# One scan call for both states of a step in every half, the norms' epsilon on GpSimd, half 0's softplus by blocks, and new places in a hand-written order

## The reference, cut to what matters

```python
dt = jax.nn.softplus(einsum('btk,kd->btd', dt, dt_proj_w) + dt_proj_b)
A_bar = exp(dt[..., None] * A)                 # 512 channels x 16 states
Bx = dt[..., None] * B_t * x_branch[..., None]
h = a * h + bx;  y = einsum('bds,bs->bd', h, c)   # for each of 1024 times
...
def _layernorm(x): return (x - mean) / sqrt(var + eps)
```

## Time and profile before

| | |
|---|---|
| three runs | 1342.04, 1348.8 (median), 1353.73 us |
| profiled execution | 1350.41 us, span 1349.1 us |
| mean granted TensorE clock | 0.959 |
| busy: PE, DVE, ACT, POOL | 1162.8, 1219.4, 818.3, 979.5 us |
| first scan | 117.3 us after the span's start |
| the eight halves, from first scan to first scan | 155.2, 149.0, 146.4, 149.0, 149.8, 149.0, 142.3 us, then 191.2 us to the end |

### The profile page before, as it was taken

The page is one execution under the profiler, slowest core; times in us unless marked ns, Lnnn a source line. Parts: engine busy times, 40 slices in busy tenths (PEclk is TensorE's granted clock), DMA queues, the critical chain, the costliest instruction groups (busy, mean ns, idle before and its releaser), DMA issues.

```text
span 1349.1 us, 12381 instructions
## 1 busy us (share of the span) xinstructions
PE 1162.8 (86%) x3574; PEld 639.5 (47%) x3574; DVE 1219.4 (90%) x1338; ACT 818.3 (61%) x1476; POOL 979.5 (73%) x528
## 2 busy tenths in 40 slices
PE   7666967998999899998899898999899899769884
PEld 5423523473446543663357443654357344423453
DVE  4656899999999999899999998899999999989976
ACT  3236645865677666955686675865686577545422
POOL 3203894799769887889679978899589978856742
PEclk9777988899999999999999999999999999989998
DMA  7305557776777669766877668776877677787811
GB/s 257 118 5 206 219 202 242 273 246 213 253 248 242 242 226 307 263 251 209 274 240 272 219 244 266 270 244 202 276 244 253 225 260 252 271 332 271 330 63 78
DMA packets 92020, 313.87 MB, mean 233 GB/s; under 512 B 10400, under 2 KB 15648, under 8 KB 91696
## 3 DMA queue, kind: packets, MB, share of 16 engines
q1 hardware_dynamic: 88928, 303.77, 64.8%
q10 hardware_dynamic: 3024, 9.31, 1.8%
HBM read 301.73 MB, written 11.31 MB: 232 GB/s over the span
## 4 chain that ended last, share of the span: by engine, by line
DVE 39%; PE 22%; issue 13%; ACT 9%; DMA 8%; POOL 8%; SPq 1%; DVEq 0%; POOLq 0%; ACTq 0%
DVE ps L1637 10%; DVE ps L1629 9%; DMA arena<-bc_scratch 7%; DVE arena L1642 6%; PE ps L844 6%; POOL arena L1851 5%; PE ps L550 4%; DVE ps L1345 4%; ACT ps L1203 3%; DVE stats_before L1238 2%; PE ps L590 1%; ACT arena L859 1%; PE ps L596 1%; PE ps L685 1%; DMA arena<-in_x 1%
## 5 line engine op out<-in xcount | busy, mean ns | idle before, releaser
L1851 POOL TENSOR_TENSOR arena<-arena 128x1024 f32<-128x1024 f32 x255 | 597.1, 2360 | 182.2 <-PE ps L844 142.6
L844 PE MATMUL ps<-arena,identF 128*128 128x512 f32 x1024 | 489.2, 610 | 50.1 <-DVE arena L1642 26.9
L1203 ACT ACTIVATE ps<-arena,negA 128x512 f32<-128x512 f32 x512 | 332.6, 683 | 102.6 <-DVE arena L1642 97.5
L1637 DVE TENSOR_TENSOR_SCAN ps<-ps,arena 128x512 f32<-128x512 f32 x258 | 316.9, 1273 | 12.1 <-ACT ps L1203 8.7
L844 PEld LDWEIGHTS ps<-arena,identF 128*128 128x128 f32 x1024 | 190.8, 194 | 283.8 <-issue 218.3
L1642 DVE TENSOR_TENSOR arena<-ps,arena 128x1024 f32<-128x1024 f32 x256 | 312.2, 1219 | 12.6 <-DMA arena<-bc_scratch 6.9
L1629 DVE TENSOR_TENSOR_SCAN ps<-ps,arena 128x1024 f32<-128x1024 f32 x127 | 290.6, 2288 | 19.6 <-ACT ps L1203 17.8
L1655 POOL TENSOR_TENSOR rnln<-vnln,consts 128x4 f32<-128x4 f32 x32 | 33.4, 1044 | 85.5 <-DVE vnln L1254 85.5
L859 ACT ACTIVATE arena<-arena,rnln 128x256 f32<-128x256 f32 x128 | 66.3, 588 | 40.1 <-POOL rnln L1657 40.0
L596 PE MATMUL ps<-arena,inw 128*128 128x512 f32 x128 | 63.9, 647 | 21.3 <-DVE arena L1351 12.1
L439 PE MATMUL ps<-identF,arena 128*128 128x128 f32 x248 | 38.6, 300 | 50.6 <-ACT arena L859 24.8
...
## 6 DMA issues: line engine op xcount, KB each, us to landing
arena<-bc_scratch SPq DMA_DIRECT2D x512, 512.0 KB, 5.0
...
```

The costliest lines, as they stand in the source:

```text
L844: x = pe.matmul(ps[:, Y, :], identF[:], inp[:, m % 4, q, :], start=False, stop=(i == BLOCK_STEPS - 1 and q == 1), skip_group_check=True)
L1203: x = act.activation(ps[:, 2 * (m % 2) + q, :], dt[:, kd, :], ACT.Exp, scale=negA[:, kd, 2 * i + q:2 * i + q + 1])
L1637: x = dve.tensor_tensor_scan(states, states, inp[:, m % 4, q, :], first, ALU.mult, ALU.add)
L1851: pool.tensor_tensor(inp[:, m % 4, :, :], u[:, kd:kd + 1, :].broadcast_to([P, 2, TH]), b_at[:, m % 3, :, :], ALU.mult).then_inc(S.inp, 1)
```

## The change

1. **Scans.** `together(m)` is gone. Every step but step 0 makes one scan of 1024 with initial value 0; step 0 makes two of 512. dt of time 0 is set to LONG in every half. The state carried into an odd half is instead multiplied by the decay of time 0 and added to time 0 of `inp`: ACT makes exp(A * dt[0]) for a pair of blocks (`act_first_decay`, two calls of 128x16, twice per odd half), POOL multiplies `carried` by it (128x32, twice per odd half), and after each `inp` of an odd half POOL adds two columns (128x2), after waiting for its own multiplication. `S.inp` is counted after that add. In all halves ACT's decay of blocks 0 and 2 waits for `S.dt_cut`, so for `u`, in odd halves for the product with `carried` too.
2. **Epsilon.** `dve_veps` is gone; `pool_rstd` makes the two small instructions itself, ahead of the power.
3. **Half 0.** x_proj comes ahead of the dt product on PE for each block. ACT makes |x|, exp and ln for blocks 0 and 1 alone, ln in two calls; DVE adds, multiplies `u` and `inp` for block 0 alone; the row loads of step 0 are split in two. Block 1's add, `u` and cut, and blocks 2 and 3's |x| (now on DVE) and relu, follow at step 1, ACT's exp at step 1 and ln at step 4, POOL's add at step 6 (before: step 4).
4. **Output loads.** Half 0 set: due at 4, 6, 8, ... 14 (before 4.25, 5.25, ... 9.25); half 1 set at 17, 19, ... 27 (before 19.25, ... 24.25); gate loads a quarter step apart.
5. **Places.** Nearly every entry of `TIMES` moves by 0.25 to 3 steps.

```diff
-    "sp_before": {"x_in": -5.75, "bc_out": 29.25, "dt_in": 29.25},
-    "sp_second": {"x_in": -21, "bc_out": 29.25, "dt_in": 29.25},
-    "sp_after": {"xr_out": 20.75, "px_out": 35.25},
+    "sp_before": {"x_in": -8.5, "bc_out": 29.25, "dt_in": 29.25},
+    "sp_second": {"x_in": -24.75, "bc_out": 29, "dt_in": 29.75},
+    "sp_after": {"xr_out": 10.75, "px_out": 38.75},
-    "pe_before": {"hn1_t0": -1.75, "hn1_t1": -1.75, "q0": -1, "k0": -1, "s0": 2, "q1": 2, "k1": 4.5, "v0": 6,
+    "pe_before": {"hn1_t0": -2.5, "hn1_t1": -2.5, "q0": -2, "k0": -2, "s0": 2, "q1": 2, "k1": 4, "v0": 5, "s1": 6,
...
-    "act_second": {"hn1": (-10, 2.25), "hB1": (2.25, 2.25), "q0": 5.75, "k0": 5.75, "q1": 8.25, "exp0a": 8.25,
+    "act_second": {"hn1": (-9, -9), "hB1": (5.5, 5.5), "q0": 5.5, "k0": 5.5, "q1": 6.75, "exp0a": 6.75,
...
-        "ffn_add": (19.5, 19.5), "ln3_rstd": 22.25, "dt_add": (35, 39), "u": (35, 39)},
+        "ffn_add": (19.5, 19.5), "ln3_rstd": 22, "dt_add": (34.5, 37.75), "u": (34.5, 38.75), "cut": (34.5, 40.5)},
...
+                if m == 0:
+
+                    sp.dma_start(b_at[:, 0, 0, :], bc_d[0, 0:1, :].broadcast_to([P, TH])).then_inc(S.first_row, 16)
+                    sp.dma_start(b_at[:, 0, 1, :], bc_d[0, 1:2, :].broadcast_to([P, TH])).then_inc(brow_in[0], 16)
+                    return
...
-            for kd in range(KD):
+            for kd in range(2):
                 x = act.activation(xb[:, kd, 0:TH], ps[:, 1, :], ACT.Abs, bias=vec("dtb", kd), scale=vec("dtw", kd))
-            x.then_inc(S.dt_abs, 1)
+            x.then_inc(S.sp_first, 1)
+            act.wait_ge(S.sp_first, 1)
+            x = act.activation(two(xb, 0)[:, :, 0:TH], two(xb, 0)[:, :, 0:TH], ACT.Exp, scale=-1.0).then_inc(S.sp_first, 1)
+            act.wait_ge(S.sp_first, 2)
+            for kd in range(2):
+                act.activation(xb[:, kd, 0:TH], xb[:, kd, 0:TH], ACT.Ln, bias=1.0).then_inc(S.sp_first, 1)
+
+            act.activation(spare_col, half_col, ACT.Exp)
+
+            yield 1
             act.wait_ge(S.dt_abs, 1)
-            act.activation(xb[:, :, 0:TH], xb[:, :, 0:TH], ACT.Exp, scale=-1.0).then_inc(S.sp_exp, 1)
+            act.activation(two(xb, 1)[:, :, 0:TH], two(xb, 1)[:, :, 0:TH], ACT.Exp, scale=-1.0).then_inc(S.sp_exp, 1)
+            yield 4
             act.wait_ge(S.sp_exp, 1)
-            act.activation(two(xb, 0)[:, :, 0:TH], two(xb, 0)[:, :, 0:TH], ACT.Ln, bias=1.0).then_inc(S.sp_ln0, 1)
             act.activation(two(xb, 1)[:, :, 0:TH], two(xb, 1)[:, :, 0:TH], ACT.Ln, bias=1.0).then_inc(S.sp_ln, 1)
...
+        def act_first_decay(h, p):
+
+            act.wait_ge(S.dt_add, 2 * h + p + 1)
+            for kd in (2 * p, 2 * p + 1):
+                x = act.activation(first_decay[:, kd % 2 * NS:(kd % 2 + 1) * NS], negA[:, kd, :], ACT.Exp, scale=dt[:, kd, 0:1])
+            x.then_inc(S.first_decay, 1)
...
-                yield t + (19.25 if hf else 4.25) + b * 2
+                yield t + (17 if hf else 4) + b * 4
...
+            elif m == BLOCK_STEPS:
+                act.wait_ge(S.first_dt, 3)
             elif kd % 2 == 0 and i == 0:
-                if g % 2:
-                    act.wait_ge(S.dt_add, 2 * g + kd // 2 + 1)
-                else:
-                    act.wait_ge(S.dt_cut, g + kd // 2 + 1)
+                act.wait_ge(S.dt_cut, 2 * g + kd // 2 + 1)
...
-        def dve_veps(site, h):
-            L = ln[site]
-            mv, vn = norm[site][1:3]
-            dve.wait_ge(L.aggr, h + 1)
-            dve.tensor_scalar(vn[:, 1, :], mv[:, :, 0], -1.0, None, ALU.mult)
-            dve.tensor_scalar(vn[:, 0, :], mv[:, :, 1], EPS, None, ALU.add).then_inc(L.veps, 1)
...
+            dve.wait_ge(S.sp_first, 3)
+            dve.scalar_tensor_tensor(dt[:, 0, :], dt[:, 0, :], 0.0, xb[:, 0, 0:TH], ALU.max, ALU.add).then_inc(S.dt_add, 1)
+            dve.wait_ge(S.dt_add, 1)
+            dve.tensor_tensor(u[:, 0, :], dt[:, 0, :], xc[:, 0, :], ALU.mult).then_inc(S.first_dt, 1)
+            dve.wait_ge(S.first_dt, 1)
+            for q in range(2):
+                dve.wait_ge(brow_in[0] if q else S.first_row, 16)
+                x = dve.tensor_tensor(inp[:, 0, q, :], u[:, 0, :], b_at[:, 0, q, :], ALU.mult)
+            x.then_inc(S.inp, 1)
+
+            dve.wait_ge(S.decay, 1)
+            dve.memset(dt[:, 0:1, 0:1], LONG).then_inc(S.dt_cut, 1)
+            yield 1
+            dve.scalar_tensor_tensor(xb[:, 2:4, 0:TH], dt[:, 2:4, :], -1.0, dt[:, 2:4, :], ALU.mult, ALU.max).then_inc(S.dt_abs, 1)
+            dve.wait_ge(S.sp_first, 4)
+            dve.scalar_tensor_tensor(dt[:, 1, :], dt[:, 1, :], 0.0, xb[:, 1, 0:TH], ALU.max, ALU.add).then_inc(S.first_dt, 1)
+            dve.wait_ge(S.first_dt, 2)
+            dve.tensor_tensor(u[:, 1, :], dt[:, 1, :], xc[:, 1, :], ALU.mult).then_inc(S.u, 1)
...
-                if m // STEPS % 2:
-                    dve.wait_ge(S.carry, STEPS * (m // STEPS // 2) + m % STEPS + 1)
-                for q in range(2):
-                    states = states_of(m)[:, q, :]
-                    first = carried[:, m % STEPS, q:q + 1] if m // STEPS % 2 else 0.0
-                    x = dve.tensor_tensor_scan(states, states, inp[:, m % 4, q, :], first, ALU.mult, ALU.add)
+
+                for q in (slice(0, 2),) if m else (slice(0, 1), slice(1, 2)):
+                    states = states_of(m)[:, q, :].rearrange("p q t -> p (q t)")
+                    x = dve.tensor_tensor_scan(states, states, inp[:, m % RING, q, :].rearrange("p q t -> p (q t)"), 0.0,
+                                               ALU.mult, ALU.add)
...
-            pool.wait_ge(L.veps, h + 1)
-            pool.tensor_tensor(rn[:, 0, :], vn[:, 0, :], neghalf, ALU.pow).then_inc(L.rstd, 1)
-            pool.wait_ge(L.rstd, h + 1)
+            mv, vn, rn = norm[site][1:]
+            pool.wait_ge(L.aggr, h + 1)
+            pool.tensor_scalar(vn[:, 0, :], mv[:, :, 1], EPS, None, ALU.add).then_inc(L.step, 1)
+            pool.tensor_scalar(vn[:, 1, :], mv[:, :, 0], -1.0, None, ALU.mult).then_inc(L.step, 1)
+            pool.wait_ge(L.step, 3 * h + 1)
+            pool.tensor_tensor(rn[:, 0, :], vn[:, 0, :], neghalf, ALU.pow).then_inc(L.step, 1)
+            pool.wait_ge(L.step, 3 * h + 3)
...
-            yield 4
+            yield 6
...
+                yield t + T["cut"][p]
+                if h % 2:
+                    own = slice(2 * p * NS, 2 * (p + 1) * NS)
+                    pool.wait_ge(S.first_decay, 2 * (h // 2) + p + 1)
+                    pool.wait_ge(S.carry, STEPS * (h // 2) + STEPS // 2 * (p + 1))
+                    pool.tensor_tensor(carried_flat[:, own], carried_flat[:, own], first_decay[:], ALU.mult).then_inc(S.to_add, 1)
+
+                pool.wait_ge(S.u, 2 * h + p + 1)
+                pool.memset(dt[:, 2 * p:2 * p + 2, 0:1], LONG).then_inc(S.dt_cut, 1)
...
+            x = pool.tensor_tensor(inp[:, m % RING, :, :], u[:, kd:kd + 1, :].broadcast_to([P, 2, TH]), b_at[:, m % 3, :, :], ALU.mult)
+            if h % 2:
+
+                x.then_inc(S.inp_part, 1)
+                pool.wait_ge(S.inp_part, STEPS * (h // 2) + m % STEPS + 1)
+                pool.wait_ge(S.to_add, 2 * (h // 2) + kd // 2 + 1)
+                x = pool.tensor_tensor(inp[:, m % RING, :, 0], inp[:, m % RING, :, 0], carried[:, m % STEPS, :], ALU.add)
+            x.then_inc(S.inp, 1)
```

More of the change, by code:

```diff
@@ new lines @@
+    "dve_after": {"ln4_stats": 6.5, "z": (6.5, 7.75, 8.5, 10.25), "ln4_moments": 6.5},
+    "pool_before": {"wo_gate": -5.5, "ffn_gate": -5.5, "ln1_rstd": -5, "ga_bias": 5, "op_add": (11.5, 11.5),
+        "ln2_rstd": 12.75, "n2a": 14, "n2b": 14, "q_scale": 16.25, "gb_bias": 17.75, "q_sub": 17.75, "q_back": 17.75,
+        "ffn_add": (19.5, 19.5), "ln3_rstd": 22, "dt_add": (34.5, 37.75), "u": (34.5, 38.75), "cut": (34.5, 40.5)},
+    "pool_second": {"ln1_rstd": 2.5, "ga_bias": 2.5, "op_add": (11.5, 11.5), "ln2_rstd": 13, "n2a": 15.25,
+        "n2b": 15.25, "q_scale": 17.25, "gb_bias": 17.25, "q_sub": 17.75, "q_back": 17.75, "ffn_add": (20, 20),
+        "ln3_rstd": 22, "dt_add": (34.5, 38.5), "u": (34.5, 41.75), "cut": (34.5, 41.75)},
@@ L99 @@
 LONG, LEAST = 1e25, 1e-20
+RING = 4
 Y, X0, X1, Y0 = 4, 5, 6, 7
@@ L119 @@
 MAMBA = ["pad", "xb_mm", "xc_init", "conv", "xc_tanh", "xc", "z_mm", "z_tanh", "z_ev", "bc_mm", "bc_sb", "dt_abs",
-         "dt_relu", "sp_exp", "sp_ln", "dt_add", "u", "dt_cut"]
-SCAN = ["decay", "carry", "inp", "scan", "prod", "dx", "y", "gated"]
+         "dt_relu", "sp_exp", "sp_ln", "dt_add", "u", "dt_cut", "first_decay", "to_add"]
+SCAN = ["decay", "carry", "inp_part", "inp", "scan", "prod", "dx", "y", "gated"]
 RECURRENT = ["cp_mm", "cp_tmp", "resA", "g_mm", "g_ev", "g_sig", "px_mm", "px", "c_f", "i_g", "c_new"]
 END = ["om", "om_bias", "fin_add", "fin_tanh", "fin_gate_pool", "fin_gate_dve", "fin_sum", "out"]
-LN = namedtuple("LN", "stats aggr veps rstd nb hn mm out")
+LN = namedtuple("LN", "stats aggr step nb hn mm out")
 SITES = ("ln1", "ln2", "ln3", "ln4")
@@ L843, in pe_scan @@
```

(6 more changed lines are left out.)

121 lines of the change are left out of this document (47 added, 74 removed), and 23 rows, old and new, of the table TIMES.

## The result

The changed kernel takes 1329.8 us by the median of 4 runs (1328.7 to 1331.1), against 1350.3 of the kernel before in the same series: ratio 0.9857, with a 95% interval of 0.981 to 0.9904. In the last series of experiments it ran again, 1329.5 against 1344.9, ratio 0.9873 (0.9851 to 0.9896). It is faster by 15 to 21 us and not by 44: inside the range (1290 to 1332), less than half of the forecast's gain.

What follows compares the result with a forecast made beforehand. It took DVE, busy 90% of the span, as the bound. From 1350.4 us, terms -21.6 - 20 - 2 - 4 - 3 + 6 + 0.8 = -43.8 gave 1306.6, stated as 1307, range 1290 to 1332.

Steps and rivals of the forecast that it cites:

- Scans: Odd halves' scan pairs: 128 pairs become single scans, each saving 0.169 us of DVE, 21.6 us off in all.
- Epsilon: At the norms: DVE's epsilon instruction waits for POOL; moving it to POOL gains 20 us, the wait not handed on.
- Rival 2: At the norms: the epsilon instruction's wait is handed on to the next one, gain 8 not 20, time 1319; chance 0.07.
- A microsecond taken off DVE is a microsecond of the span: First to last scan: DVE idles 4 to 6 us per half, so its savings shorten the span if others have room.
- Half 0 and start: Half 0's blockwise softplus: first scan about 111, 6 us earlier, partly paid back at step 1; net -2 us with norms.
- Output loads: Last half, where DVE waits for B and C rows: output loads one per two steps, -4 us (0 to -5).
- Places: Half borders and the load of x: moved places remove DVE waits, together -3 us, between -8 and +8.
- POOL late: Odd halves, steps 14 to 20: POOL's lead runs out, 1.5 us new DVE idle per odd half, +6 us in all.
- Rival 1: Middle of odd halves: POOL becomes the bound, +20 us and not +6, time 1321; chance 0.18.
- rival 3: Odd halves: POOL's small add costs 1.1 us, not 0.23, and the kernel is slower, 1367; chance 0.03.
- Rival 4: Bad places: decays behind PE waits, 1.5 us per step pair in some 20 places, +30 us, 1337; chance 0.08.
- Tail: After the last scan: the fourth exposed epsilon chain from moments to ACT, now through POOL, costs +0.8 us.

Runs made afterwards that it cites:

- `scan_only`: Kernel before with the scan part alone (one scan per step, carried state added by POOL), all places as they were: 1337.2 us, ratio 0.9932.
- `eps_psum`: Kernel before with the norms' two small epsilon instructions on POOL and the quantiser's block maxima in PSUM: 1346.5 us, ratio 0.9986.
- `eps_only`: Kernel before with the norms' two small epsilon instructions moved to POOL alone, all places as they were: 1351.6 us, ratio 1.0035.
- `eps_back`: Changed kernel with the norms' two small epsilon instructions put back on DVE, right behind the moments: 1334.4 us, ratio 0.99.
- see 7: Changed kernel with old output loads (1333.5 us), with old half 0 softplus and first row load (1333.1), with all three old (1330.25); changed kernel again 1329.5.
- `places_old`: Changed kernel's instructions with the places of the kernel before; new pieces keep own places, output loads as changed: 1348.45 us, ratio 1.0007.
- `no_add`: Changed kernel without POOL's 128 small adds of the carried state: 1323.0 us, ratio 0.9818.
- see 5: The experiment that ran the changed kernel without POOL's 128 small adds: 1323.0 us, ratio 0.9818.
- The second execution: A second profiled execution of the unaltered changed kernel: 1326.2 us.

## Why the prediction fell short

- **Scans (-21.6 and +6 for a late POOL, so -15.6)**: the durations were right to a hundredth (2.287). Alone the part gave -9.4 by the medians, -13.0 in the profile. Of DVE's 21.6, 2.5 went into the scale's wait (1.5 to 4.0 us in `scan_only`) and 5.1 into idle time.
- **Epsilon (-20) is the step that failed.** The 20 us did leave DVE (19.8 in `eps_psum`). I wrote that "the wait is the instruction's own, and is not handed on", from one place where the next instruction was a scan. That such an instruction stands until POOL's product ends was read rightly. The Trainium skill ("SBUF — State Buffer", section "Who interferes with whom") counts `tensor_scalar` among the instructions that can take the port pair that DVE shares with GpSimd. The trace agrees: the scale took 1.45 us on average beside POOL's products and 0.19 with its input in PSUM. I applied that to the instructions that go away, and not to the scale, which is of the same kind. With POOL's phase moved against DVE's, 8 us (`eps_only`) and 10 us (changed kernel) of wait came back there. Rival 2 (1319) had the wait handed on, but to the neighbour and not to another instruction 17 us later (in half 3 of before, from 603.9 to 620.8), and it was 11 us too low. The rest of the gain was cover: I costed epsilon's wait as exposed, and beside it stood PE's z product and ACT's tanh, which DVE then waits for (4.0 to 11.4 us). Measured: +5.0 with the old places, some -5 with the new.
- **"A microsecond taken off DVE is a microsecond of the span"** stood ahead of all terms and is the error behind them. I had it from DVE's idle 4 to 6 us per half. But PE, at 137 of 146.5, is nearly as full, and the z product shows a stretch where PE sets the pace. An engine that is busy 95% may wait little only because it is itself late: 16.2 us more work on DVE (`eps_back`) cost some 5 us.
- **Half 0 and start (-2)**: the first scan at 109.4 (111 was said), half 0 4.8 us longer: -3.1 in the profile. The moved work does lie beside half 1's attention, as was said (see 7). The two moved instructions that can meet POOL took 1.84 and 2.83 us where I had 1.2 and 0.7 (they took 1.21 and 0.68 in `places_old`), inside my 0 to 6.
- **Output loads (-4)**: not settled (see 7).
- **Places (-3, bounds -8 and +8)**: 19 us under the changed instructions, far outside my bounds. I priced what each moved entry mends in the kernel before. What they mend is mostly what the other parts break: POOL late (15.0 us of DVE's idle time with the old places, 5.8 with the new) and waits for ACT (44.7 and 33.2).
- **POOL late (+6)**: 6.7 by `no_add`, but not by the waits at steps 15 and 19, which the changed kernel doesn't have (see 5): the number is partly luck. Rival 1 fell (88%, not 97%), rival 3 too (0.19 us). Rival 4, bad places, is the old places' story, not the new ones'.
- **Tail (+0.8)**: +1.2.

The sum: parts 1 and 2 gave about -4 where I had -36, the places -19 where I had -3. In the profiled pair (1350.4 to 1331.1) the forecast was low by 24.5 us: 10.1 for the scale, 1.3 for the pad copy (2.3 to 3.6 us in all; that it met POOL too is likely, not shown), 11 for DVE's idle time, which grew by 9.9 where my terms made it -1 (6 - 4 - 3), and the rest for small terms. The second execution took 1326.2, and in it the idle time had grown by 4.7.
